# Projecting V ahead of normalizing K in a fused attention and quantized-FFN kernel

## The reference

```python
# x: (4, 4096, 1024), H = 16 heads of 64, LAT = 128, ROPE = 32
q  = rms_norm((x @ Wq) per head, q_g)
kv = x @ Wkv                                  # 128 latent columns
k  = rms_norm((kv @ Wk) per head of 32, k_g)
v  = (kv @ Wv) per head of 32
probs = softmax(causal(q[..., :32] @ k.T / 8))
x = layernorm(x + pad(probs @ v) @ Wo)
# FFN 1024 -> 4096 -> 1024, "bit linear": weights to {-1, 0, 1} times a scale
wq(w)   = clip(round(w / mean|w|), -1, 1) * mean|w|
x = layernorm(x + bitlinear(silu(bitlinear(x, Wg)) * bitlinear(x, Wu), Wd))
```

## Time and profile before

| | |
|---|---|
| timed runs | 4176.39 and 4188.34 us, median 4182.36 |
| the profiled execution: its time | 4182.14 us |
| its span on the slowest core (core 0) | 4180.5 us |
| spans of the 8 cores | 4153.5 to 4180.5 us |
| busy share: PE, VectorE (DVE), ScalarE (ACT), POOL | 39%, 32%, 21%, 1% |
| DMA | 278.19 MB, mean 67 GB/s |
| loads of wg and wu tiles, issue to landing | 2048 KB, 8.3 to 8.5 us (median of each group) |
| loads of wd tiles, issue to landing | 512 KB, 3.6 us |

### The profile page before, as it was taken

The page is one execution under the profiler, slowest core; times in us unless marked ns, Lnnn a source line. Parts: engine busy times, 40 slices in busy tenths (PEclk is TensorE's granted clock), DMA queues, the critical chain, the costliest instruction groups (busy, mean ns, idle before and its releaser), DMA issues.

```text
span 4180.5 us, 28989 instructions; the slowest of 8 cores (4153.5 to 4180.5 us)
## 1 busy us (share of the span) xinstructions
PE 1637.0 (39%) x8727; PEld 577.5 (14%) x8824; DVE 1324.4 (32%) x2237; ACT 862.9 (21%) x796; POOL 23.5 (1%) x75
## 2 busy tenths in 40 slices
PE   0010102221133443343454454438437464752934
PEld 0000000000011111010010010013213222321411
DVE  0233242333445554323112111132432513433252
ACT  1101101200000003352654565501001101100210
POOL 1000000000000000000000000000000000000000
PEclk8555555555556555555555555569668686876968
DMA  4434334322220000101000000033124033212402
GB/s 95 151 131 161 141 151 121 96 86 85 81 46 11 0 0 11 41 1 36 6 1 16 26 1 1 6 106 114 41 68 151 23 98 101 83 58 91 134 21 78
DMA packets 140959, 278.19 MB, mean 67 GB/s; under 512 B 7944, under 2 KB 106504, under 8 KB 134664
## 3 DMA queue, kind: packets, MB, share of 16 engines
q1 hardware_dynamic: 107256, 192.96, 13.7%
q10 hardware_dynamic: 24320, 67.12, 4.8%
q0 software_dynamic: 9232, 16.25, 2.5%
HBM read 250.61 MB, written 41.94 MB: 70 GB/s over the span
## 4 chain that ended last, share of the span: by engine, by line
PE 21%; DVE 14%; ACT 14%; DMA 7%; issue 5%; DVEq 1%; ACTq 0%; SPq 0%
ACT PTb L729 7%; ACT PT L729 6%; PE ps_f L1034 5%; PE ps_f L1040 5%; PE ps_sc L710 4%; DMA wdbuf<-scr_d 4%; PE ps_f L1121 4%; DVE xsc L1064 2%; PE ps_tf L930 1%; DMA xo_t<-xo 1%; DVE den_sb L795 1%; DVE hbuf L1076 1%; DVE hbuf L1080 1%; DVE hq L1084 1%; DMA x1f<-scr_x 1%
## 5 line engine op out<-in xcount | busy, mean ns | idle before, releaser
L710 PE MATMUL ps_sc<-qn,khat 32*128 32x512 bf16 (+3 forms) x1280 | 176.2, 533 | 384.3 <-ACT PT L729 204.6
L729 ACT ACTIVATE PT<-ps_sc,negMb 128x2048 bf16<-128x2048 f32 (+3 forms) x160 | 273.7, 1711 | 236.2 <-PE ps_sc L710 235.9
L729 ACT ACTIVATE PTb<-ps_sc,negMb 128x2048 bf16<-128x2048 f32 (+3 forms) x160 | 273.7, 1711 | 146.4 <-PE ps_sc L710 146.4
L1034 PE MATMUL ps_f<-wgbuf,xqT 128*128 128x512 bf16 x1005 | 246.6, 387 | 121.3 <-DMA wubuf<-scr_u 119.1
L1121 PE MATMUL ps_f<-wdbuf,hqT 128*128 128x512 bf16 x1000 | 253.2, 400 | 98.2 <-DMA wdbuf<-scr_d 71.3
L1040 PE MATMUL ps_f<-wubuf,xqT 128*128 128x512 bf16 x1002 | 242.5, 382 | 1.2
L737 DVE TENSOR_TENSOR PT<-PT,maskD 128x512 bf16<-128x512 bf16 x64 | 27.2, 426 | 651.8 <-ACT PT L729 651.8
L1054 DVE SCALAR_TENSOR_TENSOR hbuf<-ps_f,xsc,gate_s 128x512 f32<-128x512 f32 x128 | 96.2, 751 | 401.1 <-ACT gate_s L1048 401.1
L296 ACT ACTIVATE wqbuf_s<-wfbuf_s 128x1024 bf16<-128x1024 f32 (+1 forms) x48 | 91.7, 1910 | 391.9 <-DMA wfbuf_s<-wdT 151.6
L930 PE MATMUL ps_tf<-ident,hq 128*128 128x128 bf16 x512 | 71.8, 301 | 228.8 <-DVE hq L1084 214.4
L1048 ACT ACTIVATE gate_s<-ps_f,xsc 128x512 f32<-128x512 f32 x128 | 87.9, 687 | 345.5 <-PE ps_f L1040 345.5
(11 more groups left out here) (224 smaller groups left out, 2242.2 us busy)
## 6 DMA issues: line engine op xcount, KB each, us to landing
wgbuf<-scr_g SPq DMA_DIRECT2D x32, 1024.0 KB, 5.5
wubuf<-scr_u SPq DMA_DIRECT2D x32, 1024.0 KB, 8.1
wfbuf_s<-wgT SPq DMA_DIRECT2D x8, 2048.0 KB, 8.4
wfbuf_s<-wgT ACTq DMA_DIRECT2D x8, 2048.0 KB, 8.4
wfbuf_s<-wuT SPq DMA_DIRECT2D x8, 2048.0 KB, 8.3
wfbuf_s<-wuT ACTq DMA_DIRECT2D x8, 2048.0 KB, 8.5
wfbuf_s<-wdT SPq DMA_DIRECT2D x32, 512.0 KB, 3.6
wfbuf_s<-wdT ACTq DMA_DIRECT2D x32, 512.0 KB, 3.6
```

The lines of the kernel that those rows point to most:

```text
L710: e.matmul(ps_sc[:, j * 512 + stc:j * 512 + 512], khat[32 * j:32 * j + 32, gi * T + sc * 128: gi * T + sc * 128 + 128], qn[32 * j:32 * j + 32,
L729: mk_exp = P.emit(s, lambda e, stc=stc, pp=pp: e.activation(PTr[pp][:, :, stc:512], PSr[:, :, stc:512], AF.Exp, bias=negMb[:, 0:1]), waits ...
L1034: P.emit(t, lambda e, c=c, i4=i4, bi=bi, gb=gb: e.matmul(ps_f[:, gb:gb + 512], xqT[:, i4 * D + c * 128:i4 * D + c * 128 + 128], wgbuf[bi][ ...
```

## The change

The V group is moved ahead of the khat group, whole, with its four `f0_step(1)` calls. The khat group then stands last in the round. Nothing else is changed; the lines are those of the kernel before, only in another order.

```diff
                         f0_step(1)                       # after the chain
                         for hc in range(NHC):
+                            pvp = ps_a if hc % 2 == 0 else ps_b
+                            vb = hc % 2
+                            w9 = []
+                            if mk_vread[vb] is not None:
+                                w9.append(mk_vread[vb])
+                            mk9 = P.emit(t, lambda e, hc=hc, s0=s0, pvp=pvp: e.matmul(
+                                pvp[:], wv_sb[:, hc * 128:(hc + 1) * 128],
+                                kvT[:, s0:s0 + 512], start=True, stop=True),
+                                waits=w9, incs=[(cT, 1)])
+                            mk10 = P.emit(v, lambda e, pvp=pvp: e.tensor_copy(
+                                vtbuf[:], pvp[:]), waits=[(cT, mk9[1])], incs=[(cV, 1)])
+                            mk_vread[vb] = mk10
+                            for ss in range(4):
...
+                            P.emit(v, lambda e, c5=c5, hc=hc: e.tensor_copy(
+                                vtok.rearrange("p (a n) -> p a n", n=512)
...
+                                waits=[(cT, cT.v)], incs=[(cV, 1)])
+                            f0_step(1)
+
+                        for hc in range(NHC):
                             co = hc * T + s0
                             P.emit(t, lambda e, hc=hc: e.matmul(
                                 ps_bc[:], bch[hc][:], chainh[:],
...
                                 kmax2[:, hc:hc + 1], kmax2[:, hc:hc + 1], sm4[:, 0:1]),
                                 incs=[(cV, 1)])
                             f0_step(1)
-                        for hc in range(NHC):
-                            pvp = ps_a if hc % 2 == 0 else ps_b
...
-                            f0_step(1)
-
                     f0_step(200)
```

More of the change, by code:

```diff
@@ L454, in build_nc @@
                         for hc in range(NHC):
+                            pvp = ps_a if hc % 2 == 0 else ps_b
[11 more added lines that the diff above has]
+                            for ss in range(4):
+                                w = [(cV, mk10[1])] if ss == 0 else []
+                                P.emit(t, lambda e, ss=ss: e.transpose(
+                                    ps_vt[:, ss * 128:(ss + 1) * 128],
+                                    vtbuf[:, ss * 128:(ss + 1) * 128], ident[:]),
+                                    waits=w, incs=([(cT, 1)] if ss == 3 else []))
+                            P.emit(v, lambda e, c5=c5, hc=hc: e.tensor_copy(
+                                vtok.rearrange("p (a n) -> p a n", n=512)
+                                [:, 4 * c5:4 * c5 + 4, hc * 128:hc * 128 + 128],
+                                ps_vt.rearrange("p (a n) -> p a n", n=128)),
+                                waits=[(cT, cT.v)], incs=[(cV, 1)])
+                            f0_step(1)
+                        for hc in range(NHC):
                             co = hc * T + s0
```

## The result

The changed kernel took 4190.47 us (median of 43 runs, 4181.37 to 4209.97) against 4181.5 us (median of 42, 4174.11 to 4196.74): +9.0 us. The ratio of the two is 1.0021, 95% interval 1.0015 to 1.0027, so it is slower by 0.2%, and within 2%. The forecast was +6.8 us.

A forecast was written before the change was run, and what follows sets the result against it. The first 1240 us were taken to be a chain of latencies with no engine full. The terms 0 + 0.2 - 0.6 + 8.1 - 0.9 summed to +6.8 us, so 4189 us, range 4177 to 4203.

The forecast's parts named there:

- The first stage is a chain of latencies, and a block counts where it outlasts its cover: First 1240 us: no engine is full; a block's time counts only where it outlasts what the chain waits for anyway.
- Round 4, +8.1: khat replaces V around the scale step and two 512 KB quantizing steps: +8.1 us, the term that decides.
- The bare pair around the scale step: Round 4, blocks beside steps 67 and 68 with no store to hide under: khat for V costs 1.05 + 2.28 us.
- Rounds 0 and 1, -4.56 and +4.56: Bare blocks around the scale step: round 0 swaps khat for V, saving 4.56 us; round 1 does the reverse; they cancel.
- 2 MB steps 12 to 14 (+0.2): Round 0, khat instead of V, nearly covered by the 1 MB store: +0.2 us in all, bounds 0 and 1.
- Round 7, -0.9: No weight step left; khat 0's ps_bc wait of 1.33 shrinks to about 0.4: -0.9 us, bounds 0 and -1.3.
- Round 2, -0.6: absacc memset and two x loads start 1.1 us earlier, competing less with the first wd load: -0.6 us.
- rival 1: Round 2: earlier x loads get further ahead, a second wd load is stuck: +4.8 us, so 4194 us; chance 0.14.
- Rounds 3, 5, 6 at nothing: Round 3 is all absolute steps; in 5 and 6 both groups stand in quantizing steps before and after: 0 us.
- The rest of the kernel: Stages behind 1240 us: no change in length by more than a few us; the first stage's delay arrives at the end.
- The clock rival: FFN matmuls: the shift leaves a tenth more at the lower clock, 4270 us or more, or 4100 or less; 0.02 each.
- The rival in two_halves: Follow-up's rival: shared memory saturates, 2 MB loads take over 12 us, gain stops at about -300 us, ratio 0.928; no chance given.

The follow-up runs named there:

- two-buffer kernels: 512 KB wd tiles alternate between two quarters of the buffers, in old order and with V ahead of khat everywhere; 3983.83 and 3992.07 us.
- db_old: Old order, 512 KB wd tiles alternating between two buffer quarters, against the kernel before: 3983.83 us, ratio 0.9552.
- two_halves: Two-quarter wd buffers, wg and wu tiles in halves, relaxed ps_bc wait, absacc memset on VectorE, freer x load, V first in rounds 0 and 7; 3727.24 us, ratio 0.8930.
- r4_only: V ahead of khat in round 4 alone, old order elsewhere, against the kernel before: 4188.22 us, ratio 0.9997 (0.9972 to 1.0021).
- not_r4: V ahead of khat in every round except round 4, against the kernel before: 4184.63 us, ratio 0.9992 (0.9964 to 1.0020).
- r07_only: V ahead of khat in rounds 0 and 7 alone, against the kernel before: 4176.09 us, ratio 0.9973 (0.9946 to 0.9999).
- zv_new: V ahead of khat in all rounds, absacc memset on VectorE instead of POOL, against the kernel before: 4175.23 us, ratio 1.0002.
- zv kernels: absacc memset on VectorE instead of POOL, in old order (4167.14 us, ratio 0.9983) and with V ahead of khat (4175.23 us, ratio 1.0002).
- bc_old: Old order, first ps_bc matmul of khat 1 to 3 waiting only for ps_bc's last reader, against the kernel before: 4158.83 us, ratio 0.9975.

## Why the prediction was right, step by step

- **The first stage is a chain of latencies, and a block counts where it outlasts its cover.** Right. More cover gone makes the order cost nothing in round 4 (0.7 us in the two-buffer kernels), a shorter block makes it cost less (4.7), and letting loads and stores run under the work takes 189 us (db_old) and, with the other changes of two_halves, 446 us off a kernel whose work stays the same.
- **Round 4, +8.1, the deciding term.** Measured +8.7 after and +7.9 in r4_only. The bare pair around the scale step cost 9.32 - 5.89 = 3.43 for the expected 3.33, and the two periods 2.4 and 2.6 (after) or 2.3 and 2.3 (r4_only) as the mean of the cores, for the expected 2.40 each.
- **Rounds 0 and 1, -4.56 and +4.56.** -5.2 and +4.8. The stretches are 5.79 and 10.54 on core 3, next to 5.89 and 10.45 read from the other order. The small cost put on the 2 MB steps 12 to 14 (+0.2) did not show beside it; it was at the bottom of its bounds.
- **Round 7, -0.9.** -1.7 after, -1.5 in not_r4, -0.8 in r07_only as the mean of the cores. The row that I had to guess, what is left of the wait for `ps_bc` of khat 0, reads 0.43 where I had put 0.4, and this core's stretch from the chain's end to the last `kmax2` is 25.38 us, where it was 26.63 to the last `vtok`: -1.25, at the edge of the bound given. It ends at 1242.68, 8.3 us after the 1234.43 of core 0 before, for the 7 that were forecast.

```profile
1216.61 0.69 DVE L451 TENSOR_TENSOR chainl<-rkfull,chainh 128x512 bf16<-128x512 f32 x1
1217.41 0.69 DVE L464 CAST vtbuf<-ps_a 128x512 bf16<-128x512 f32 x1
...
1226.24 0.75 DVE L489 SCALAR_TENSOR_TENSOR khat<-krall,kg_sb,ps_bc 128x512 bf16<-128x512 bf16 x1 [0.43 <-PE ps_bc L486]
...
1242.53 0.15 DVE L501 TENSOR_TENSOR kmax<-kmax,sm 4x1 f32<-4x1 f32 x1
```

- **Round 2, -0.6.** Wrong in sign: +2 us in the three steps that the x loads meet. The failed step is "If their bytes are done 1.1 sooner, the round gains up to 1.1". I read it from core 0 alone, which already paid for the collision in full, and half of the cores did not. It was akin to rival 1, with a smaller price than the 4.8 us I gave it and at another load: no second load is stuck, but the first one is, on all cores. As the mean of the cores the first tile takes 3.4 us more, and 1.4 us of it come back on the second; single cores lose up to 7 us on the first, and core 0 gains 1.3. The rule of the Trainium skill (DMA: Bandwidth & Descriptors, "Issuing engines are not separate DMA queues") that loads of all issuers interleave on the same engines was borne out, by the wd load that landed in 7.6 to 10.1 us with the x loads ahead of it (after) and in 3.5 to 4.3 without them (zv_new); that the sum would stand by it was not, since the wd load that comes to wait is on the chain and the x loads are not.
- **Rounds 3, 5, 6 at nothing.** +0.7, +1.4, +0.1 after, but also 143.3 to 146.5 for round 5 in kernels that have it in the old order: noise between executions.
- **The rest of the kernel.** Untouched, as forecast: query projection 358.0 and 358.2 us, granted clock 0.77 in the last stretch of both, and from `negMb` to the end 2580.7 and 2578.2 us. The clock rival had no part. A sum of the measured rounds is +10.7, the runs say +9.0, the forecast was +6.8, and most of what it lacks is the wrong term of round 2; with rounds that scatter by 1 to 3 us in a single execution I can't say more of the difference.

## What to carry to other kernels

A block slipped into a serial chain costs only what it outlasts of the wait beside it, so before two blocks of different length are exchanged, list for each what stands around it: here the same exchange cost 8 us, gave back 5, or did nothing, by the step that it fell beside. Look at what stands behind an instruction in its queue when it moves, on all cores and not only on the slowest. And where such cover decides anything, the chain itself is the thing to change: splitting the one tile buffer in two for wd alone brought 189 us, and for all three weights, with some smaller changes, 446 us, fifty times what the order moved.

## What was not expected of the hardware

- A 512 KB load issued behind two 2 MB loads from another queue: where it was issued under 0.1 us after the first of them, it landed in 3.5 to 4.1 us, as without them (3.4 to 4.3 in the zv kernels); 0.4 to 0.6 us after it, in 5.1 to 7.2; 0.65 us, in 8.2 (bc_old), and 0.72 us, in 8.4 (core 0 before); 1.1 us and more, in 7.5 to 10.7. Less than a microsecond of lead decides it.
- With all 8 cores loading nearly all the time, each still moved 242 to 248 GB/s over a stretch of 140 us (200 to 340 us of two_halves, DMA share 0.74 or 0.75), the rate of one 2 MB tile in 8.4 us before (some 250 GB/s). The rival in two_halves that counted on a saturation of the memory they share fell. Whether the 8.4 us are already those of 8 cores at once was not tested, since no run has one core alone.
- In the first 340 us of two_halves the granted clock of TensorE is given as 1.00, the level of 2.4 GHz, on the profiled core (core 1), while its 128x512 matmuls last 0.59 to 0.63 us, as they do later where the clock is given as 0.50 to 0.52, and as they do on core 2 in the same stretch at 0.51 to 0.52. No time was gained by it; what it means was not looked into.
